# One wait fewer ahead of the second half of the final gathers in a perceiver block

## The reference

```python
x = x + xattn(layernorm(x), ctx)       # softmax(ctx . x) over 1601 keys, then times ctx
x = x + attn(layernorm(x), ...)        # 8 heads of 128, with position terms
h = layernorm(x); h = h + mla(rmsnorm(h), ...)   # 16 heads of 32, causal, 64 rows
x = x + h + moe(rmsnorm(h), ...)       # one shared expert and 7 routed ones
```

```python
scores, idx = top_k(sigmoid(xt @ W_router + bias), 2); scores = scores / sum(scores)
hmid = silu(xt @ Wg_r[e]) * (xt @ Wu_r[e])
out  = shared + sum over the two picked e of scores[e] * (hmid @ Wd_r[e])
```

## Time and profile before

| | |
|---|---|
| time, median of 3 executions | 846.12 us (844.21 to 847.1) |
| the profiled execution's own time | 844.21 us |
| its span, from the first to the last instruction | 842.4 us |
| busy share of the span: PE, DVE, ACT, POOL | 95%, 62%, 36%, 36% |
| share of PE in the chain that ended last | 87% |

### The profile page before, as it was taken

One profiled execution on the slowest core, in us unless ns is written; L12 is line 12 of the kernel. 1 busy time (PEld: TensorE's weight loads), 2 busy tenths in 40 slices (PEclk: granted clock), 3 DMA queues, 4 the chain that ended last, 5 costly groups with the idle time before them and its releaser, 6 DMA issues.

```text
span 842.4 us, 16057 instructions
## 1 busy us (share of the span) xinstructions
PE 803.4 (95%) x6098; PEld 596.3 (71%) x6099; DVE 518.9 (62%) x1162; ACT 307.3 (36%) x830; POOL 306.2 (36%) x152
## 2 busy tenths in 40 slices
PE   4899999999899999999999999999989999999993
PEld 4555455554557689888877777688868888888882
DVE  5878977798752345637688878864373343344336
ACT  4322233133442136663148665823313211211211
POOL 0000000000443624545022121343719999994033
PEclk9999999999999999999999999999999999999997
DMA  9958655783520040012159100040465554441147
GB/s 357 384 205 313 252 201 211 278 311 115 213 101 1 1 153 1 1 43 90 48 212 384 57 0 1 1 151 1 176 228 191 195 199 160 158 165 50 50 121 253
DMA packets 46425, 127.02 MB, mean 151 GB/s; under 512 B 3984, under 2 KB 8080, under 8 KB 40224
## 3 DMA queue, kind: packets, MB, share of 16 engines
q1 hardware_dynamic: 36896, 106.03, 34.4%
q10 hardware_dynamic: 6912, 11.80, 4.0%
q0 software_dynamic: 2560, 8.39, 3.0%
HBM read 102.05 MB, written 24.15 MB: 150 GB/s over the span
## 4 chain that ended last, share of the span: by engine, by line
PE 87%; DVE 6%; issue 2%; ACT 2%; POOL 1%; DMA 1%; another core or an unknown queue 1%; SPq 0%; DVEq 0%; POOLq 0%
PE scores L567 10%; PE bank L600 10%; PE bank L1121 7%; PE bank L1119 7%; PE bank L1120 7%; PE bank L534 2%; PE bank L657 2%; PE bank L828 2%; PE bank L659 2%; PE bank L732 2%; PE bank L829 2%; PE bank L658 2%; PE bank L834 2%; PE bank L734 2%; PE bank L733 2%
## 5 line engine op out<-in xcount | busy, mean ns | idle before, releaser
L1783 DVE STREAM_TRANSPOSE ctxT<-nat 128x1024 f32<-128x1024 f32 (+3 forms) x124 | 116.7, 1003 | 0.9 <-DMA nat<-in_ctx_keys 0.7
L600 PE MATMUL bank<-nat,probT 128*64 128x512 f32 (+1 forms) x416 | 94.4, 597 | 0.1
L1332 POOL TENSOR_TENSOR ring_lo<-ring_raw,ring_hi 128x2048 fp32r<-128x2048 f32 x18 | 83.0, 4612 | 19.7 <-ACT ring_hi L1685 18.5
L567 PE MATMUL scores<-ctxT,hn 32*64 32x385 f32 (+5 forms) x2048 | 88.4, 487 | 1.8 <-issue 1.0
L1218 POOL TENSOR_TENSOR wq_lo<-wq_raw,wq_hi 128x1024 fp32r<-128x1024 f32 x4 | 9.5, 2400 | 220.5 <-ACT wq_hi L1431 220.5
L567 PEld LDWEIGHTS scores<-ctxT,hn 32*64 32x64 f32 x2048 | 62.9, 131 | 24.3 <-issue 12.9
L1119 PE MATMUL bank<-ring_hi,xg_lo 128*128 x176 | 72.6, 413 | 0.0
L1121 PE MATMUL bank<-ring_hi,xg_hi 128*128 x176 | 69.0, 392 | 0.0
L1120 PE MATMUL bank<-ring_lo,xg_hi 128*128 x176 | 68.5, 389 | 0.0
L600 PEld LDWEIGHTS bank<-nat,probT 128*64 128x64 f32 (+1 forms) x416 | 28.8, 136 | 52.9 <-issue 51.4
L2414 DVE TENSOR_TENSOR rhm_lo<-bank,rhm_hi 128x512 fp32r<-128x512 f32 x22 | 15.2, 693 | 82.3 <-ACT rhm_hi L1696 78.7
(11 more groups left out here) (305 smaller groups left out, 1898.7 us busy)
## 6 DMA issues: line engine op xcount, KB each, us to landing
nat<-in_ctx_keys SPq DMA_DIRECT2D x48, 1024.0 KB, 7.1
ring_raw<-in_Wexp SPq DMA_DIRECT2D x21, 1024.0 KB, 6.6
x_slots<-zeros SPq DMA_DIRECT2D x1, 5632.0 KB, 18.3
y_slots<-zeros SPq DMA_DIRECT2D x1, 5632.0 KB, 32.8
hn<-x_slots ACTq DMA_DIRECT2D x22, 256.0 KB, 3.1
y_slots<-hn ACTq DMA_DIRECT2D x22, 256.0 KB
w_raw<-in_Wexp SPq DMA_DIRECT2D x3, 1024.0 KB, 5.0
nat<-in_ctx_keys SPq DMA_DIRECT2D x16, 130.0 KB
```

The source lines that it names most:

```text
L567: last = nc.tensor.matmul(scores4[64 * b:64 * b + 64, i, 0:keys_in[i]], q4[rows_i, j, 64 * b:64 * b + 64], ctxT[rows_i, b, j, 0:keys_in[i] ...
L600: last = nc.tensor.matmul(bank[7][64 * b:64 * b + 64, :], probT[0:n, j, 64 * b:64 * b + 64], nat[k % 2][0:n, b, j, :], start=j == 0, stop= ...
L1332: last = nc.gpsimd.tensor_tensor(ring_lo[at], ring_raw[at], ring_hi.bitcast(F32)[at], ALU.subtract)
L1783: dve.transpose(dst, src).then_inc(columns_ready, 1)
```

## The change

The wait on `rup_full` between the two halves of the gathers is taken out. The wait for the stores ahead of the first gather stays, and so does everything else. The 16 gathers are then issued one after the other, in the same order.

```diff
@@ -1339,8 +1339,6 @@
             pool.sem_inc(used_stored, 1)
             pool.wait_ge(used_stored, 1)
             for k in range(NT):
-                if k == NT // 2:
-                    pool.wait_ge(rup_full, TILES)
                 for i in range(2):
                     nc.gpsimd.indirect_dma_start(picked[2 * k + i][:], None, y_slots,
                                                  bass.IndirectOffsetOnAxis(slots[:, k, i:i + 1], 0)).then_inc(picked_loaded[picked_part(k)[0]], 16)
```

## The result

The changed kernel is slower. Its median is 855.71 us (854.98 to 857.39, 5 runs), that of the kernel before 846.12 (844.21 to 847.1, 5 runs); the ratio is 1.0118, with a 95% interval of 1.0103 to 1.0134. The forecast was 845.6, with a range of 843.6 to 847.3. The profiled execution took 852.74 us.

What follows compares the result with a forecast made beforehand. The prediction took DVE with its 16 additions to bound the tail, POOL within half a microsecond of it. On the median of 846.12 us, a gain of 0.47 gave 845.65, stated as 845.6, with a range of 843.6 to 847.3.

Steps and rivals of the forecast that it cites:

- gap of 0.30 us ahead of gather 9: POOL between gathers 8 and 9: idle time falls from 2.01 to 0.30 us, 1.71 us less.
- the last pair: DVE's last two additions of picked rows: start at 837.96 instead of 838.43, without the 0.38 us wait for their gather.
- the chain: The tail's chain of waits: would go through DVE's additions, its last split, ACT and PE instead of POOL's gathers.
- rival A: Tail: the whole 1.77 us on the chain of waits comes off, 844.35 on the median; chance 0.02.
- B: Last gather's landing: full DMA engines keep it near 838.4, so nothing comes off, 846.1; chance 0.06.
- the forecast gain: End of the kernel: 0.47 us off, because DVE's last pair of additions starts that much earlier.
- nothing moves on SP, ACT, PE or DVE: Step on what changes: one POOL wait goes, and all that moves is the issue of eight gathers.
- Could the earlier gathers cost something elsewhere?: Step on side costs to other engines or POOL's issue pace: nothing that the end sees, taken as zero.
- What the wait protects: Step on the wait's purpose: it held gathers 9 to 16 until tile 22's up product; no data need it.
- Rival C: DVE's last-tile product and split held up by POOL's gathers: at most 1.4 us slower, 847.5; chance 0.04.
- the four cases: The forecast of 0.3 to 0.7 us off (chance 0.88), rival A, B and Rival C; none reaches 0.3% (2.5 us).
- the 0.91: Chance given to the whole kernel's time staying the same, within 0.3%; faster had 0.05, slower 0.04.

Runs made afterwards that it cites:

- c1_after: The changed kernel, unaltered, run again as a control on chip 6: ratio 0.9976 to the kernel before.
- r9: The kernel before with 16 extra plain loads from POOL's queue, one every 1.37 us, on chip 6: ratio 1.0.
- r10: The kernel before with 16 extra unbroken gathers of half rows inside the loop over tiles, on chip 6: ratio 0.9989.
- s10: The kernel before with 16 extra unbroken gathers of half rows inside the loop over tiles, on chip 11: ratio 1.0175.
- e4: The kernel before with 16 extra unbroken gathers of whole rows inside the loop over tiles, on chip 8: ratio 1.0142.
- e1: The changed kernel with three waits added on idle SP, for tile 22's gate and up products and tile 21's down product: 853.83 us, one run.
- e10: The kernel before with 16 extra unbroken gathers of half rows inside the loop over tiles, on chip 13: ratio 1.0012.
- s11: The changed kernel with POOL memsets of 0.97 us after gathers 5 and 10, on chip 11: ratio 1.0002 to the kernel before.
- r11: The changed kernel with POOL memsets of 0.97 us after gathers 5 and 10, on chip 6: ratio 0.9982 to the kernel before.
- e11: The changed kernel with POOL memsets of 0.97 us after gathers 5 and 10, on chip 13: ratio 0.9994 to the kernel before.
- e12: The kernel before with one POOL memset of 1.8 us after scatter 5 of its 16 scatters, on chip 13: ratio 1.0035.

## Why the prediction was wrong

**What held.** The gap of 0.30 us ahead of gather 9; gather 9 at 10.06 us after gather 1 (forecast 821.68 - 811.62 = 10.06); gather 16 after 18.81 us (forecast 19.19; no additions ran beside it to stretch it; with them, in c1_after, 19.51). That the last pair had no wait, and that the gathers were off the chain, held in the first measurement for the wrong reason: DVE was 9 us late, and everything had landed. In c1_after they held for the reason that was given. There the chain goes through DVE's additions, its last split, ACT and PE; the first addition comes 16.19 us after gather 1 (16.20 in before, so rival A is refuted), and the last pair has no wait (so B is).

The last pair of c1_after starts 833.77 - 807.43 = 26.34 us after gather 1, and that of the kernel before 838.43 - 811.62 = 26.81: 0.47 us, the forecast gain to the hundredth. That it fits so well is luck, since both times come from one execution each, and from different chips. In the eleven other profiles with the tail of before, the last pair starts 26.46 to 27.38 us after gather 1, with a wait of 0 to 0.97 us; the two of them on the chip of c1_after have 26.46 (r9) and 26.96 (r10), so the tail gains 0.1 to 0.6 us there. The measured 2.0 us (0.3 to 3.6) contains this at its lower edge; what the rest would be is open, and may be spread.

**The step that failed** is "Could the earlier gathers cost something elsewhere?", which ends in "the upper bound is nothing that the end sees; I take zero", and the sentence ahead of it, that "nothing moves on SP, ACT, PE or DVE". The argument followed data: who reads from a DMA, who waits for a gather. What was disturbed are the completions of an engine that has no part in the transfers. From gather 1 to DVE's first addition it cost 9.6 us in the place of 0, on the chip of the first measurement, where the silu, DVE's product and ACT's copy came 8.5, 11.5 and 8.9 us late. On chip 6 the step held.

**The row was there.** To bound the cost of 16 indirect DMAs in a row, the prediction took POOL's own durations beside the scatters, found them even, and stopped. Just behind them stood DVE's 7.18 us "<-remote", and PE idle for 0.93, 0.32 and 1.41 us. The last silu, with 4.49 us "<-remote", stood in the very stretch under study; it was hidden, since PE took up DVE's product only after tile 21's down product. The precedent was looked up, but only on the engine that issues.

**What the wait protects** was answered for data alone ("nothing else in the code takes over the role of the wait"). It also cut the stream into two parts of 8 gathers, 10 us each. A completion is on time 3.9 us into an unbroken stream (s10) and 5.3 us into it (after: the copy at 816.33). The next ones seen are late: 2.4 us for a product that ended 6.9 us into the stream (e4: 776.17, silu at 778.52), 2.9 us for one at 7.0 (s10: 778.42, silu at 781.35). The last counts get through 1.7 to 3.0 us after the stream ends (823.03 - 821.38 before, 794.28 - 791.26 in s10). Time in the stream alone doesn't give the delay, though: beside the scatters of before a product that ended 11.9 us in (603.16) was taken up only 0.86 us late (604.02). Two halves cost a hidden delay; one whole costs 9.1 us. (The wait ahead of gather 1 has at most 811.62 - 808.67 = 2.95 us between store and gather, where the prediction says some 2; that the three later tiles are padding stands.)

**Rival C** had the sign, with 0.04, and the wrong mechanism: neither the product nor the split was held by a gather on POOL (both took 0.69 us). The product was released late, and the split followed it. Its bound of 1.4 us came from the mechanism, so it could not have held the time.

**The chances.** "None of these cases reaches 0.3%" was true of the four cases and of no others. The chance for a case not thought of was left at the spread of runs. With the rows above, read as a precedent, it would have had to carry a good part of the 0.91.

**Chip by chip.** The unaltered changed kernel has a ratio on two chips only: +1.2% in the first measurement, where the remote waits show, and -0.2% (-0.4% to 0) on chip 6, where they don't. On chip 8 it ran once, with the three waits of e1 added (853.83 us, median of before 847.25), and had the remote waits. The kernel before is itself slower on the chips that show them: 847.25, 847.01 and 846.87 us, against 843.71 on both others. PE's idle times behind the scatters in its profile, 0.93 + 0.32 + 1.41 = 2.66 us, would be most of this; in c1_after and e10 PE has none there.

**What stays open.** Where the completions are held. The Trainium skill, Perfetto Trace Analysis, section Tensor Engine Instruction (MATMUL, LD_WEIGHTS), says that a matmul's end in the profile is an estimate, and that its semaphore is updated only when PSUM has acknowledged the writes, and then has to spread to all engines. No run here shows the two steps apart. PE went on at 0.23 us a matmul for 5 us, and another engine's completion came through on time: in e4, 16 us into the scatters, ACT's silu, itself released late (7.24 us "<-remote"), ended at 608.98, and DVE's product behind it began at 609.01. This fits a late acknowledgement, and a late spreading of PE's counts alone. Nor is it known whether other streams of POOL's than indirect DMAs do it, what differs between the chips, or whether it always holds for a chip: one chip (number 11) was seen twice, with the effect both times.

No version beat both kernels on every chip. The changed kernel is the faster one on chip 6 and was 1.2% slower in the first measurement; with short breaks it costs nothing that was measured on three chips (s11, r11, e11), and gains nothing.

## What to carry to other kernels

Before taking a wait out, look at what ran on all engines the last time that the same instructions went without a break, above all for idle times whose releaser has no name: here they were there, 200 us earlier. A wait that protects no data can still be a pause that something else lives on; try a plain pause in its place, at another point too. And a null result needs a control on the same chip that shows that the effect could have appeared.

## What the runs showed of the hardware

- On chips 8 and 11, and in the first measurement, an unbroken stream of POOL's indirect DMAs (one in 1.25 us) made PE's completions reach ACT, DVE and SP late, by 8.5 to 11.7 us at the end of the changed kernel (after, e1); with 256 KB and with 128 KB a gather the price was alike (1.0142 and 1.0175). On chips 6 (changed kernel, 16 extra gathers of 128 KB) and 13 (the extra gathers) they were on time within 0.04 us. Sixteen plain loads by SP at a DMA share of 0.89 did nothing of the kind on chip 11.
- POOL's scatters, 0.96 us each, took 1.89 to 2.98 us beside DVE's TENSOR_TENSOR with two inputs in SBUF (4.49 us for two, e12). The Trainium skill, SBUF — State Buffer, section Who interferes with whom, infers that such an instruction takes only the read side of the shared ports, and that descriptor generation needs the write side. Here the issue of an indirect DMA is stretched all the same. It also reads its row numbers (`slots`) from SBUF, and no run tells this reading from the writing of descriptors.
